# Where the last texts leave their banks: the seam between the cross-attention of the last pair and the first expert round

## The reference

```
x = layernorm(x + attention(x))        # 16 heads, causal
x = layernorm(x + cross(x, ctx))       # slots = x; 3 rounds of:
    sn = rmsnorm(slots) @ Wq.T ; scores = sn . k_proj * D**-0.5
    attn = softmax(scores over the slots); attn /= attn.sum(-1) + 1e-6
    slots = gru_cell(attn @ v_proj, slots)
x = layernorm(x + experts(x))          # 16 experts of 64, top 4 of sigmoid(x @ sel.T)
    hidden = relu(x @ keys[e]); out = sum over the 4 of gate[e] * hidden @ values[e]
```

## Time and profile before

| | us |
|---|---|
| median of 3 runs | 652.57 (649.79 to 653.44) |
| profiled execution | 653.15 |
| its span | 651.4 |
| PE busy in the span | 619.9 (95%) |
| DVE busy | 491.0 (75%) |
| ACT busy | 326.6 (50%) |
| POOL busy | 229.1 (35%) |
| mean granted clock of PE | 0.991 |

### The profile page before, as it was taken

The page is one execution under the profiler, slowest core; times in us unless marked ns, Lnnn a source line. Parts: engine busy times, 40 slices in busy tenths (PEclk is TensorE's granted clock), DMA queues, the critical chain, the costliest instruction groups (busy, mean ns, idle before and its releaser), DMA issues.

```text
span 651.4 us, 13981 instructions
## 1 busy us (share of the span) xinstructions
PE 619.9 (95%) x5064; PEld 564.7 (87%) x5080; DVE 491.0 (75%) x1037; ACT 326.6 (50%) x734; POOL 229.1 (35%) x276
## 2 busy tenths in 40 slices
PE   8989999999989899999999999999999997999996
PEld 7767777787779899999999999999999986999995
DVE  4565677677746888979888798887998988667653
ACT  5434555555764456573555745566465644131220
POOL 9603435243453431332313323133222115161542
PEclk9799999999999999999999999999999999899999
DMA  9545567365200400000000000000000000132250
GB/s 314 156 131 173 154 190 210 108 202 175 62 18 1 162 2 2 17 18 1 0 0 16 16 0 0 0 0 0 0 2 2 1 1 1 51 115 85 81 162 33
DMA packets 31710, 43.34 MB, mean 67 GB/s; under 512 B 3408, under 2 KB 19248, under 8 KB 31664
## 3 DMA queue, kind: packets, MB, share of 16 engines
q1 hardware_dynamic: 31392, 42.47, 20.9%
q10 hardware_dynamic: 272, 0.26, 0.1%
HBM read 29.39 MB, written 13.21 MB: 65 GB/s over the span
## 4 chain that ended last, share of the span: by engine, by line
PE 65%; DVE 14%; issue 13%; POOL 4%; ACT 3%; another core or an unknown queue 0%; DVEq 0%; POOLq 0%; ACTq 0%
PE bank L449 28%; PE bank L2172 11%; PE bank L1984 4%; PE bank L1884 3%; POOL hid_hl L797 3%; PE bank L1842 2%; PE bank L1849 2%; PE bank L1865 2%; PE bank L457 2%; PE bank L2001 2%; PE bank L1970 1%; PE bank L1869 1%; PE bank L1851 1%; DVE attn L1380 1%; PE bank L1993 1%
## 5 line engine op out<-in xcount | busy, mean ns | idle before, releaser
L449 PE MATMUL bank<-slots_hl,whhT_hl 128*128 128x256 f32 x864 | 113.2, 284 | 0.0
L449 PEld LDWEIGHTS bank<-slots_hl,whhT_hl 128*128 128x128 f32 x864 | 105.7, 188 | 2.4 <-ACT gate_z L1101 1.0
L2172 PE MATMUL bank<-attn_hl,vg_hl 128*128 128x256 f32 x864 | 105.5, 280 | 0.2
L2172 PEld LDWEIGHTS bank<-attn_hl,vg_hl 128*128 128x128 f32 x864 | 100.7, 188 | 4.4 <-ACT attn_hl L811 3.9
L1290 DVE TENSOR_REDUCE neg_max<-bank 128x2 f32<-128x512 f32 (+1 forms) x96 | 65.5, 690 | 42.1 <-PE bank L1851 28.5
L867 ACT ACTIVATE pT<-bank 128x512 f32<-128x512 f32 x96 | 56.9, 598 | 44.5 <-PE bank L1865 29.0
L688 POOL TENSOR_TENSOR sq<-sq 128x256 f32<-128x256 f32 x24 | 18.1, 754 | 170.5 <-ACT sq L1086 130.2
L674 POOL TENSOR_SCALAR_AFFINE_SELECT pT<-pT 128x512 f32<-128x512 f32 x64 | 40.4, 636 | 100.6 <-ACT pT L867 100.6
L449 PE MATMUL bank<-values_hl,hid_hl 128*128 128x256 f32 x384 | 49.4, 287 | 0.3 <-DVE x L1560 0.3
L797 POOL TENSOR_TENSOR hid_hl<-hid,hid_hl 128x512 fp32r<-128x512 f32 x32 | 40.9, 1303 | 24.7 <-ACT hid_hl L811 24.6
L449 PE MATMUL bank<-x2T_hl,keys_hl 128*128 128x256 f32 x384 | 48.6, 284 | 0.0
(11 more groups left out here) (216 smaller groups left out, 1300.6 us busy)
## 6 DMA issues: line engine op xcount, KB each, us to landing
gate_rows<-gate_mem SPq DMA_DIRECT2D x48, 128.0 KB, 3.0
q_rows<-q_hl SPq DMA_DIRECT2D x21, 256.0 KB, 2.8
k_rows<-k_hl SPq DMA_DIRECT2D x21, 256.0 KB, 2.6
q_op<-q_rows SPq DMA_DIRECT2D x28, 192.0 KB, 3.2
k_op<-k_rows SPq DMA_DIRECT2D x14, 384.0 KB, 4.4
x_in<-in_x_dram SPq DMA_DIRECT2D x8, 256.0 KB, 3.1
c_in<-in_ctx_dram SPq DMA_DIRECT2D x8, 256.0 KB, 2.8
out_dram<-y_out SPq DMA_DIRECT2D x8, 256.0 KB, 2.7
```

Of the source, the lines that this page charges most:

```text
L449: mm = pe.matmul(dst, left(a), right(b), start=first and n == 0, stop=last and n == 2, skip_group_check=True)
L2172: mm = pe.matmul(halves(b)[:, m, :], vg_hl[:, j, v_part, 3 * t + r, q:q + P], attn_hl[:, j, at_part, t, :], start=n == 2 and a + m + t == ...
```

## The change

- ACT copies each raw turned text of the last pair out of its bank into `x2` (`raw_text`, semaphore `raw_ok`): the first in place of the exponentials of the last unit, the second at the head of the first expert round. Moments and norms then read `x2`, and the norm is written in place.
- PE turns the first of them in the midst of the products of the last unit, between `xn` and `z`, instead of ahead of all of them.
- In unit 4 of the last pair DVE does `totals` and `weights` for unit 5 ahead of `diff` and `slots`.
- In the first round PE turns the texts of pair 1 directly from `x2`, and the copies to `x2f` are left out there.
- `FIRST_ORDER` changes: `tT` 0 goes to the front, `tT` 1 and `lg` 0 go ahead of `gb` 4 to 7. The jobs in front of which PE waited for `x2_ok` now wait for `raw_ok`.
- DVE does both sets of moments after `gated(7)`, ahead of the routing of the next pair's text 0; `last_norm(0)` comes behind that, `last_norm(1)` in the norm of the first result. POOL's two roots go behind its eight remainders. ACT's order in the first round follows.

```diff
--- before.py
+++ after.py
@@ -300,7 +300,7 @@
         uu_ok, uT_mm = event("uu_ok", 2), event("uT_mm", 2)
         var2, rstd2, x2_ok = event("var2", 2), event("rstd2", 2), event("x2_ok", 2)
 
-        xf_ok = event("xf_ok", 2)
+        raw_ok, xf_ok = sem("raw_ok"), event("xf_ok", 2)
         tT_mm, tT_hi, tT_lo = event("tT_mm", 2), event("tT_hi", 2), event("tT_lo", 2)
         lg_mm, lg_ok, lT_mm, lx_ok = event("lg_mm", 2), event("lg_ok", 2), event("lT_mm", 2), event("lx_ok", 2)
 
@@ -417,8 +417,8 @@
                         ("half", 0), ("lT", 0), ("o", 0), ("lg", 1), ("gT", 0), ("half", 1), ("lT", 1), ("o", 1),
                         ("h", 0), ("gT", 1), ("h", 1), ("h", 2), ("h", 3)]
 
-        FIRST_ORDER = [("gb", 0), ("gb", 1), ("h", 4), ("h", 5), ("gb", 2), ("h", 6), ("gb", 3), ("second gT", 1), ("h", 7), ("gb", 4), ("tT", 0),
-                       ("gb", 5), ("tT", 1), ("gb", 6), ("lg", 0), ("gb", 7)] + EXPERT_ORDER[7:]
+        FIRST_ORDER = [("tT", 0), ("gb", 0), ("gb", 1), ("h", 4), ("h", 5), ("gb", 2), ("h", 6), ("gb", 3), ("h", 7), ("second gT", 1),
+                       ("tT", 1), ("lg", 0), ("gb", 4), ("gb", 5), ("gb", 6), ("gb", 7)] + EXPERT_ORDER[7:]
         AHEAD = (("tT", 0), ("tT", 1), ("lg", 0), ("lT", 0), ("lg", 1), ("gT", 0), ("lT", 1), ("gT", 1), ("h", 0), ("h", 1), ("h", 2), ("h", 3))
 
         FIRST_TEXT = (1, 3)
@@ -431,6 +431,7 @@
 
         FIRST_FREE = {("h", n): (4 + n % 2, h_relu, due(8, 0, n - 1)) for n in range(4, 8)}
         FIRST_FREE |= {("gb", n): (6 + n % 2, h_ok, due(8, 0, n - 1)) for n in range(8)}
+        FIRST_FREE |= {("tT", 0): (0, raw_ok, 1), ("tT", 1): (1, gT_lo, due(2, 0, 1)), ("half", 0): (2, raw_ok, 2)}
         FIRST_FREE |= {("h", n): (4 + n, h_relu if n < 2 else h_ok, due(8, 0, n % 2 + 7)) for n in range(4)}
 
         def bank_free(jobs, i, key, final=False):
@@ -788,7 +789,6 @@
             with pool.Fori(0, PAIRS - 1) as i:
                 cross(i)
             cross(PAIRS - 1, last=True)
-            rstd(PAIRS - 1, var2, rstd2, std2[:, 0], 1, 0)
             def experts(i, first=False):
                 for j in range(2):
                     for g in range(4):
@@ -796,8 +796,9 @@
                         pool.wait_ge(h_hi, due(8, i, n + 1))
                         pool.tensor_tensor(hid_hl[:, j, LO, 2 * g:2 * g + 2, :], hid[:, n % HIDDEN, :, :],
                                            f32(hid_hl[:, j, HI, 2 * g:2 * g + 2, :]), ALU.subtract).then_inc(h_lo, 1)
-                        if first and n == 4:
-                            rstd(PAIRS - 1, var2, rstd2, std2[:, 1], 2, 1)
+                if first:
+                    for j in range(2):
+                        rstd(PAIRS - 1, var2, rstd2, std2[:, j], j + 1, j)
                 for j in range(2):
                     rstd(i, var3, rstd3, std3, j + 1, j)
             experts(0, True)
@@ -1077,6 +1078,10 @@
                 act.wait_ge(h_mm, due(8, i, 4 * j + 4, back=1))
                 copy(x2T_hl[:, j, HI, :, :], halves(b)).then_inc(tT_hi, 1)
 
+            def raw_text(j):
+                act.wait_ge(uT_mm, due(2, PAIRS - 1, j + 1))
+                copy(x2[:, 2 * NT * (PAIRS - 1) + j * NT:2 * NT * (PAIRS - 1) + (j + 1) * NT, :], halves(LAST_TEXT[j])).then_inc(raw_ok, 1)
+
             def cross(i, last=False):
                 def start(u):
 
@@ -1112,6 +1117,8 @@
                     reset_gate(u)
                     if u + 1 < UNITS or not last:
                         soft(i, u + 1)
+                    else:
+                        raw_text(0)
                     gates(u)
                     if u + 2 < UNITS:
                         start(u + 2)
@@ -1183,17 +1190,18 @@
                     act.wait_ge(o_mm, due(2, i, j + 1, back=1))
                     copy(hid_hl[:, j, HI, 2 * g:2 * g + 2, :], hid[:, n % HIDDEN, :, :]).then_inc(h_hi, 1)
                 if first:
+                    raw_text(1)
+                    expert_text_hi(i + 1, 0, 0)
                     hidden_hi(0)
                     hidden_hi(1)
                     relu(i, 4)
                     relu(i, 5)
+                    relu(i, 6)
+                    hidden_hi(2)
                     gates_hi(1)
-                    hidden_hi(2)
+                    relu(i, 7)
                     hidden_hi(3)
-                    relu(i, 6)
                     hidden_hi(4)
-                    relu(i, 7)
-                    expert_text_hi(i + 1, 0, 0)
                 else:
                     for n in range(4):
                         hidden_hi(n)
@@ -1622,8 +1630,8 @@
 
             def last_moments(j):
                 counted, links[0] = links[0], 2 * j
-                dve.wait_ge(uT_mm, due(2, PAIRS - 1, j + 1))
-                moments(0, last_chain, 0, lambda t: halves(LAST_TEXT[j])[:, t, :], stats2[:, j * NT:(j + 1) * NT],
+                dve.wait_ge(raw_ok, j + 1)
+                moments(0, last_chain, 0, lambda t: x2[:, 2 * NT * (PAIRS - 1) + j * NT + t, :], stats2[:, j * NT:(j + 1) * NT],
                         mv2[:, j * NT:(j + 1) * NT], std2[:, j], var2)
                 links[0] = counted
 
@@ -1643,11 +1651,13 @@
                     if u + 1 < UNITS or not last:
                         soft_sum(i, u + 1)
                     if last and u == UNITS - 1:
-                        last_moments(0)
                         logits(0, 0, FIRST_TEXT[0])
                         logits(0, 1, FIRST_TEXT[1])
                     if last and 0 < u < 5:
                         expert_weights_lo(2 * u - 1)
+                    if last and u == 4:
+                        totals(i, u + 1)
+                        weights(i, u + 1)
                     dve.wait_ge(n_ok, due(UNITS, i, u + 1))
 
                     before = x1T[:, :, bass.ds(i * (2 * T) + j * T, T)] if u < 2 else slots[:, j, :, :]
@@ -1681,11 +1691,12 @@
                     gates(u)
                     if u == 4 and not last:
                         context_text_lo(i, 0)
-                    if u + 1 < UNITS:
+                    ahead = last and u == 4
+                    if u + 1 < UNITS and not ahead:
                         totals(i, u + 1)
                     if u + 2 < UNITS:
                         mean_square(i, u + 2, 0)
-                    if u + 1 < UNITS:
+                    if u + 1 < UNITS and not ahead:
                         weights(i, u + 1)
                     if u + 1 < UNITS - 1:
                         attn_lo(i, u + 1)
@@ -1730,7 +1741,7 @@
             cross(PAIRS - 1, last=True)
 
             def last_norm(j):
-                normal(PAIRS - 1, lambda t: halves(LAST_TEXT[j])[:, t, :], mv2[:, j * NT:(j + 1) * NT], std2[:, j], rstd2, j + 1,
+                normal(PAIRS - 1, lambda t: x2[:, 2 * NT * (PAIRS - 1) + j * NT + t, :], mv2[:, j * NT:(j + 1) * NT], std2[:, j], rstd2, j + 1,
                        lambda t: x2[:, 2 * NT * (PAIRS - 1) + j * NT + t, :], x2_ok)
 
             def text(i, j):
@@ -1764,31 +1775,24 @@
                 elif not last:
                     text(i + 1, 0)
                 gated(2)
-                if first:
-                    last_norm(0)
-                    gates_lo(0, 1, FIRST_TEXT[1])
-                elif not last:
+                if not (first or last):
                     text(i + 1, 1)
                 gated(3)
+                if not last:
+                    expert_text_lo(i + 1, 0, 0)
                 if first:
-                    text(1, 0)
-                    text(1, 1)
-                if not (first or last):
-                    expert_text_lo(i + 1, 0, 0)
-                gated(4)
-                if first:
-                    last_moments(1)
-                gated(5)
-                if first:
-                    expert_text_lo(i + 1, 0, 0)
-                gated(6)
-                if first:
-                    last_norm(1)
-                gated(7)
+                    gates_lo(0, 1, FIRST_TEXT[1])
+                for n in range(4, 8):
+                    gated(n)
                 if not last:
                     logits(i + 1, 0, 0)
                     expert_text_lo(i + 1, 1, 1)
+                    if first:
+                        last_moments(0)
+                        last_moments(1)
                     route(i, i + 1, 0)
+                    if first:
+                        last_norm(0)
                     logits(i + 1, 1, 1)
                 for j in range(2):
                     if j and not last:
@@ -1799,6 +1803,8 @@
                     dve.wait_ge(u3_ok, due(2, i, j + 1))
                     dve.wait_ge(stored[j], due(1, i, 1, back=1, step=16))
                     moments(i, expert_chain, EXPERT_LINKS, lambda t: u3[:, t, :], stats3, mv3, std3, var3)
+                    if first and j == 0:
+                        last_norm(1)
                     normal(i, lambda t: u3[:, t, :], mv3, std3, rstd3, j + 1, lambda t: y_out[:, j, t, :], y_ok)
                 assert last or links[0] == 2 * EXPERT_LINKS_BEFORE + EXPERT_LINKS
```

(20 more changed lines are left out.)

## The result

| | before | changed |
|---|---|---|
| median of 11 runs each, same chip | 652.57 us (649.79 to 655.76) | 647.79 us (646.75 to 651.57) |
| profiled execution, its span | 653.15, 651.4 | 649.62, 647.9 |
| mean granted clock in it | 0.991 | 0.995 |

The ratio is 0.9938 (95% interval 0.992 to 0.9956). A second set of 7 runs gave 648.45 us and 0.995 (0.9929 to 0.9971). The forecast was 648.3.

A forecast was written before the change was run, and what follows sets the result against it. PE, busy 95% of the span, was taken as the bound, with holes and a slow-clock stretch in the seam. Of 6.9 us gained 2.6 are given back, leaving 4.3: 648.3 us from the median, range 645.8 to 651.3.

The forecast's parts named there:

- Part 1: Unit 4, last pair: totals and weights first; products with `attn_hl` start 1.92 us earlier, logits net 1.14 us.
- Part 2: Last unit and first round: two raw-text copies on ACT, 0.63 us each at most, hidden.
- Part 3: First round: `x2f` copies (0.85 us of DVE) and PE's wait for them go; turning text 0 costs nothing.
- Part 4: First round: values start at 548.3 instead of 553.58, 5.3 us gained; clock staying up brings another 1.5.
- Part 5: Next text's turned gates: late DVE routing leaves a 2.6 us hole, 4.3 us gained of 6.9; `std` loses 0.9.
- Part 6: After those gates: norms take 1.5 us of DVE, 0 to 0.4 to lose; PE dense, gain stays.
- Sum: Whole kernel: span 651.4 less 4.3 is 647.1; 648.85 us profiled, 648.3 from the median; chance 0.44.
- the fall of the clock in the new wait: PE's clock falls in the new 2.6 us hole: price 1.5 us, time 649.8, chance 0.27.
- DVE becomes the bound: First round: DVE's idle time can't take 5.2 us of added work; no gain, 652.5 us, chance 0.09.
- The slow case: Two long clock falls, from 545 to 548 and in the wait for the gates, cost 6.8: 655.1 us, chance 0.05.

The follow-up runs named there:

- e5: e4 with the remainder of attn for unit 5 done by DVE behind the first diff instead of by POOL; 646.18 us, ratio 0.9914.
- e6: Kernel before with the raw copies alone, moments and norms on `x2`, PE waiting on `raw_ok`; 652.12 us, ratio 1.001.
- e7: Kernel before without the two `x2f` copies of the first round, all else as before; 650.94 us, ratio 0.9965.
- e11: Changed kernel with both moments at their old places, those of text 1 between `gated(4)` and `gated(5)`; 652.47 us, ratio 0.997.
- e3: Changed kernel with both sets of moments behind the routing of the next pair's text 0; 648.47 us, ratio 0.9935.
- e4: Changed kernel with moments in DVE's idle stretches: text 0's ahead of unit 5's logits, text 1's ahead of the next text 1's remainder; 648.18 us, 0.9931.
- e1: Changed kernel with diff and slots again ahead of totals and weights in unit 4 of the last pair; 651.83 us, ratio 0.9963.
- e2: Kernel before with only totals and weights moved ahead of diff and slots; 655.83 us, ratio 1.004.
- e10: e9 with ACT's exponentials left in their bank, where DVE's first routing instruction reads them instead of `prb`; 646.01 us, ratio 0.9895.
- e9: e5 with only text 1's statistics at the idle place, their aggregation and `std` behind the routing of text 0; 644.91 us, ratio 0.9893.
- e8: Changed kernel with `tT` 1 and `lg` 0 back at their old places between gate products 4 to 7; 648.68 us, ratio 0.9933.

## Why the prediction held, step by step

- **Part 1** was the main mis-sized term. The products with `attn_hl` start 1.87 us earlier in the seam (5.78 for 7.65), forecast 1.92. But POOL's remainder took 1.72 us and not the 1.28 I had put down from a row in which DVE was idle: beside it DVE now runs `diff`, with two inputs in SBUF. The logits gained 0.56 instead of 1.14 (11.32 for 11.88), and the wait for the remainder cost PE 0.80 instead of the 0.39 in the sum. e5 shows it: with the remainder on DVE the logits come 0.80 earlier, from the same start of the products (5.78). The price of this lock stood in part 5 and was missing in part 1.
- **Part 2** held: the raw copies took 0.60 and 0.57 us, and nothing waited for them. e6 shows that freeing the banks is worth nothing by itself.
- **Part 3** held; e7 gives the copies' worth as 1.1 in the old kernel's seam.
- **Part 4**: the values start 4.5 us earlier in the seam, forecast 5.3; 0.58 of the shortfall is part 1's. Of the 4.54, part 1 gives 0.56, the copies 1.06 (e7) and the moments 2.04 (e11). The other 0.9 no run isolates; the two norms of L1560, 0.99 and 0.98 us in the kernel before, left DVE's list ahead of `gated(7)` too. The clock stayed up in both traces of the changed kernel.
- **Part 5** held: hole of 2.23 for a forecast of 2.6, one `std` of 0.90 for 0.93. e3 and e4 show what it stands for: the bound has gone from PE to DVE's list in this round.
- **Part 6** held up to the seam's end: no wait at the turned gates of text 1. Its last step, that PE is dense from there and the gain stays, failed: 0.85 us went later, above all in the third round's wait of 1.38 (0.43 before).
- **Sum**: 3.78 us in the seam for 4.3 forecast, 649.62 us for 648.85 in the profiled execution, and -4.8 in the median. That these lie near each other is in part luck: the later rounds gave back 0.85, the changed execution happened to enter the seam 0.57 earlier, and the forecast took the clock's worth from one execution with one fall of 1.5 us in its seam, while the mean loss over the runs went down by 1.4 to 2.1. Which hole that goes with stays open: the loss is 5.9 in e1, where the hole of 2.61 is gone and that of 1.57 is back, 5.8 in e6 and 4.4 in e7, which have both holes or nearly so.
- **Rivals**: the fall of the clock in the new wait was seen once, in e1, and not in the two traces of the changed kernel. "DVE becomes the bound" was half right: it is the bound, but not at a price that eats the gain (its three terms add up to 5.1 us, not 5.2, which changes nothing). The slow case did not occur; only e2 came out slower, by a longer wait with a fall behind it, beside the fall that the kernel before had too. The rule of the Trainium skill on the shared port (SBUF — State Buffer, "Who interferes with whom") agrees with e10, 1.36 against 0.19, and should have been applied to part 1.

A version that beats both kernels came out of it: e9 at 0.9893 and e10 at 0.9895, 644.91 and 646.01 us. Their intervals overlap; e10 has the shorter seam and the smaller rest.

## What to carry to other kernels

When an edit takes work off an engine's list ahead of a wait, find where that work lands: it is cheapest in that engine's idle stretches (e4), and in a full list it moves the wait (e3). When instructions change places on DVE or POOL, price each by what the other one now does beside it. And judge edits of a microsecond by a stretch between two fixed instructions in the traces, with the clock's falls set apart; medians alone would have put e4 level with the changed kernel and e11 with the one before.

## What the runs showed of the hardware

- **The same wait, with and without a fall of the clock.** 2.61 us idle before the logits brought a fall in the trace of before; 2.60 at the same place in e6's did not. 2.23 did in e1 and did not in the changed kernel. Both fit the rule of the Trainium skill cited ahead, that the gate's watching isn't aligned to the kernel (TensorE: Matmul & The Clock Gate, Part 1); no run here shows the gate's own timing.
- **The shared port works both ways**: POOL's remainder went from 1.28 to 1.72 us beside DVE's `diff`, and DVE's `slots` from 0.69 to 1.65 beside the remainder. A small DVE product in the routing of text 1 (`gate`, 128x32) took 1.16 us beside POOL's remainders in the traces of both kernels, where the same instruction of text 0's routing took 0.19. So the engines do not meet only by semaphores, as the opening has it. The statistics with inputs in SBUF kept their 0.37 us each beside POOL's run (0.73 or 0.74 for two).
- **A small write landed late in five of fourteen traces, and the third round then waited.** SyncE's list of the changed kernel and of before (columns: start, time, what is issued):

```profile
588.59 5.14 SPq L593 DMA_DIRECT2D gate_rows<-gate_mem  x8
```

```profile
589.90 0.33 SPq L587 DMA_DIRECT2D gate_mem<-gateT  x1
592.35 5.14 SPq L592 DMA_DIRECT2D gate_rows<-gate_mem  x8
```

From the write of the gates (585.27 in the changed kernel) to the reads that wait for it: 3.32 us there and 2.45 before. It was 3.3 to 3.6 in five of the traces (changed twice, e7, e8, e11), and all five then wait 1.26 to 1.38 us at a turned gate of the third round; in the others it was 1.5 to 2.6 and that wait 0.62 at most. In the changed kernel the link shows in DVE's list too: a `hid` of the third round (L1769, at 602.56) waits 1.10 us for the DMA of `gate_rows`. Why the landing differs was not tried.
